# First attention to second layer, taken by halves: the first half of the tokens projected, added and normalised ahead of the second; weight peaks read in eight parts

## The reference

```
h = patches @ W_lin + b, class token, positions                # embedding
z = layernorm(h)
z = z + global_attention(rmsnorm(z, norm1_w))                   # "first attention", 16 heads, latent keys and values, rope
z = z + local_attention(rmsnorm(z, norm2_w))                    # "second layer" of the same block, 4 key heads, rope
h = h + z
n = layernorm(h);  h = h + routed experts(n) (32, best 8) + 2 shared experts(n)
h = h + attention(layernorm(h))                                 # dense, 16 heads
n = layernorm(h);  h = h + quantised MLP(n)
```

## Time and profile before

| what | us |
|---|---|
| median of three runs | 369.97 (368.08 to 370.18) |
| the profiled execution | 369.53 |
| its span, first to last instruction | 367.7 |
| TensorE busy | 348.3 (95%) |
| VectorE busy | 234.3 (64%) |
| ScalarE busy | 192.7 (52%) |
| POOL busy | 135.3 (37%) |

### The profile page before, as it was taken

One profiled execution on the slowest core, in us unless ns is written; L12 is line 12 of the kernel. 1 busy time (PEld: TensorE's weight loads), 2 busy tenths in 40 slices (PEclk: granted clock), 3 DMA queues, 4 the chain that ended last, 5 costly groups with the idle time before them and its releaser, 6 DMA issues.

```text
span 367.7 us, 9982 instructions
## 1 busy us (share of the span) xinstructions
PE 348.3 (95%) x3975; PEld 297.9 (81%) x3975; DVE 234.3 (64%) x507; ACT 192.7 (52%) x384; POOL 135.3 (37%) x144
## 2 busy tenths in 40 slices
PE   8999899998988999999999999999999999889985
PEld 6856666686667999999999999999998688666653
DVE  4546889797769366565556555555555572765787
ACT  5267954686574444445544544445444785232473
POOL 0046752372251356666555544544420012320000
PEclk9999999999999999999999999999999999999999
DMA  8930001000550434353555454544300000000001
GB/s 290 398 139 1 4 4 30 1 4 4 175 173 0 139 112 141 114 151 136 144 150 152 151 141 121 141 142 145 101 0 2 0 2 4 4 6 0 3 0 68
DMA packets 14866, 32.09 MB, mean 87 GB/s; under 512 B 2480, under 2 KB 4464, under 8 KB 14576
## 3 DMA queue, kind: packets, MB, share of 16 engines
q1 hardware_dynamic: 13328, 30.48, 26.0%
q10 hardware_dynamic: 1504, 1.13, 0.9%
HBM read 30.91 MB, written 0.69 MB: 86 GB/s over the span
## 4 chain that ended last, share of the span: by engine, by line
PE 73%; DVE 10%; ACT 8%; issue 5%; DMA 1%; SPq 1%; POOL 1%; POOLq 0%; DVEq 0%; ACTq 0%
PE psum L1172 73%; DMA km<-in_experts 1%; ACT region L797 1%; DVE xn L835 1%; ACT sq L580 1%; ACT region L789 1%; DVE rc L896 1%; SPq L376 1%; DVE nt L830 1%; ACT L567 1%; DVE nt L832 1%; DVE xc L821 1%; ACT region L648 1%; DVE rc L907 1%; ACT ars L583 1%
## 5 line engine op out<-in xcount | busy, mean ns | idle before, releaser
L1172 PE MATMUL psum<-xh,split_all 128*128 128x296 f32 x544 | 122.1, 299 | 0.0
L487 POOL TENSOR_TENSOR split_all<-km,split_all 128x768 fp32r<-128x768 f32 x34 | 62.7, 1848 | 82.0 <-ACT split_all L689 82.0
L1172 PEld LDWEIGHTS psum<-xh,split_all 128*128 128x128 f32 x544 | 91.6, 188 | 0.1
L1172 PE MATMUL psum<-xl,split_all 128*128 128x296 f32 (+1 forms) x288 | 85.1, 300 | 0.6 <-POOL xl L530 0.6
L710 ACT ACTIVATE ah<-rt 128x296 fp32r<-128x296 f32 x64 | 28.9, 452 | 72.9 <-DVE rt L1030 66.2
L1172 PEld LDWEIGHTS psum<-xl,split_all 128*128 128x128 f32 (+1 forms) x288 | 53.1, 187 | 1.6 <-POOL xl L530 1.0
L1172 PE MATMUL psum<-ah,split_all 128*128 128x296 f32 x272 | 48.6, 300 | 1.7 <-ACT ah L710 1.6
L1032 DVE TENSOR_TENSOR al<-rt,ah 128x296 fp32r<-128x296 f32 x60 | 28.7, 478 | 31.1 <-ACT ah L710 31.1
L1027 DVE TENSOR_TENSOR rb<-psum,wb 128x296 f32<-128x296 f32 x60 | 27.9, 466 | 25.1 <-ACT psum L708 24.9
L1172 PEld LDWEIGHTS psum<-ah,split_all 128*128 128x128 f32 x272 | 40.6, 188 | 2.6 <-ACT ah L710 2.0
L1030 DVE TENSOR_TENSOR rt<-rb,psum 128x296 f32<-128x296 f32 x60 | 27.7, 462 | 5.7 <-DVE rb L1027 1.7
(11 more groups left out here) (195 smaller groups left out, 562.8 us busy)
## 6 DMA issues: line engine op xcount, KB each, us to landing
km<-in_experts SPq DMA_DIRECT2D x34, 384.0 KB, 4.0
wb<-weights SPq DMA_DIRECT2D x32, 296.0 KB, 3.7
w_sb<-in_w SPq DMA_DIRECT2D x2, 1024.0 KB, 8.3
region<-in_x SPq DMA_DIRECT2D x6, 296.0 KB, 4.8
region<-in_w_lin ACTq DMA_DIRECT2D x6, 128.0 KB, 5.3
qkv_sb<-in_qkv_w SPq DMA_DIRECT2D x1, 768.0 KB, 4.7
cst<-in_consts SPq DMA_DIRECT2D x1, 502.5 KB, 7.2
out<-x SPq DMA_DIRECT2D x2, 148.0 KB, 1.8
```

The costliest lines, as they stand in the source:

```text
L487: nc.gpsimd.tensor_tensor(wl[i], ring[i], wh[i].bitcast(f32), ALU.subtract)\
L1172: return nc.tensor.matmul(out_, lhsT, rhs, start=start, stop=stop, skip_group_check=True)
```

## The change

The output projection of the first attention is done by halves. The first half's is issued ahead of the value sums of the last pair, into banks 2 and 3; VectorE adds it ahead of the last normalisation. The variance of that half, the projection of the second half (into banks 0 and 1) and eight products for warmth on either side stand in place of `norm(1)`. The second half is squared on ScalarE ahead of `qk_units(1)`; its variance is issued by TensorE after the mean square of unit 0, its root by ScalarE in turn 1 after that turn's copy and square, and its norm is applied by VectorE at the end of turn 1. Each addition is one instruction over both chunks instead of two. The peaks of w1 and w2 are read in eight parts of 512 columns: two after the last normalisation, three after the second half's addition, two and one behind the additions of the second attention, and a small reduction joins them. The core of the diff:

```diff
+PEAK_PARTS = 4
+            def stream_squares(hf):
+                act_e.wait_ge(s_x0, hf + 1)
+                nc.scalar.activation(sq[:, :, half(hf)], x0[:, :, half(hf)], ACT.Square).then_inc(s_sq, 1)
+            def stream_rsqrt(hf):
+                act_e.wait_ge(s_var, 2 + hf + 1)
+                link(nc.scalar.activation(ars[:, half(hf)], ps[2 + hf][:, 0:HALF], ACT.Abs_reciprocal_sqrt,
+                                          bias=eps[:, 2:3]))
+                nc.scalar.activation(nt[:, half(hf)], ars[:, half(hf)], ACT.Square).then_inc(s_ars, 1)
...
+                    if a == 1 and u == 1:
+                        stream_rsqrt(1)
                     if u >= 1:
                         m = n - 1
...
                 if a == 1:
-                    norm(1, mean=False, eps_at=2)
+                    load_table(ACT.Abs_reciprocal_sqrt)
+                    stream_squares(0)
+                    stream_rsqrt(0)
+                    stream_squares(1)
                 qk_units(a)
...
-            def weight_peak(k, w):
-                nc.vector.tensor_reduce(pk[:, k:k + 1], w[:], AX.X, ALU.max, apply_absolute_value=True).then_inc(s_pk, 1)
+            def weight_peak(k, part):
+                n = C * FF // PEAK_PARTS
+                nc.vector.tensor_reduce(pkp[:, k, part:part + 1], (w1_sb, w2_sb)[k][:, part * n:(part + 1) * n], AX.X,
+                                        ALU.max, apply_absolute_value=True).then_inc(s_pkp, 1)
+            def weight_peaks():
+                dve.wait_ge(s_pkp, 2 * PEAK_PARTS)
+                nc.vector.tensor_reduce(pk[:, 0:2], pkp[:], AX.X, ALU.max).then_inc(s_pk, 2)
...
                         ins.then_inc(s_kmv, 1)
+                    if a == 1 and u == 1:
+                        norm_apply(1, 4, 2, (1,))
...
+            def stream_added(hf):
+                dve.wait_ge(s_wo, hf + 1)
+                dve.wait_ge(s_x0s, hf + 1)
+                nc.vector.tensor_tensor(x0[:, :, half(hf)], x0[:, :, half(hf)],
+                                        psum[:, 2 - 2 * hf:4 - 2 * hf, 0:HALF], ALU.add).then_inc(s_x0, 1)
...
-                if a == 1:
-                    norm_apply(1, 4, 2)
                 qk_units(a)
+                if a == 0:
+                    for p in range(PAIRS - 1):
+                        normalise_grouped(0, p)
+                    stream_added(0)
+                    normalise_grouped(0, PAIRS - 1)
+                    dve.wait_ge(s_ffw, 32)
+                    weight_peak(0, 0)
+                    weight_peak(0, 1)
+                    norm_apply(1, 4, 2, (0,))
+                    stream_added(1)
+                    weight_peak(0, 2)
+                    weight_peak(0, 3)
+                    weight_peak(1, 0)
+                    continue
...
-                    ins.then_inc((s_x0, s_h)[a], 1)
-                if a == 0:
-                    weight_peak(1, w2_sb)
+                    ins.then_inc(s_h, 1)
+                    if hf == 0:
+                        weight_peak(1, 1)
+                        weight_peak(1, 2)
+                    else:
+                        weight_peak(1, 3)
+                        weight_peaks()
...
                     exchange(a, u)
+                    if a == 1 and u == 0:
+                        pe.wait_ge(s_x0, 2)
                     head_mean_squares(a, u)
+                    if a == 1 and u == 0:
+                        stream_variance(1)
...
-            def project_grouped(a):
-                for hf in range(2):
-                    pe.wait_ge(s_on, a * PAIRS + PAIRS // 2 * (hf + 1))
+            def project_grouped(a, hf):
+                pe.wait_ge(s_wo_w, 16 * (a + 1))
+                pe.wait_ge(s_on, a * PAIRS + PAIRS // 2 * (hf + 1))
...
+            def stream_variance(hf):
+                pe.wait_ge(s_sq, 2 + hf + 1)
+                for c in range(C):
+                    ins = mm(ps[2 + hf][:, 0:HALF], const("mean"), sq[:, c, half(hf)], c == 0, c == C - 1)
+                ins.then_inc(s_var, 1)
...
+                        if p == PAIRS and a == 0:
+                            project_grouped(0, 0)
                         grouped_values(a, p - 1)
...
                 if a == 1:
-                    norm(1, mean=False)
+                    keep_busy(7, 8)
+                    stream_variance(0)
+                    project_grouped(0, 1)
+                    keep_busy(7, 8)
                     pe.wait_ge(s_attn_w[1], 48)
                 qk_units(a)
```

More of the change, by code:

```diff
@@ L204, in program @@
         pk1 = sb("pk1", [P, 4])
+        pkp = sb("pkp", [P, 2, PEAK_PARTS])
         scale = sb("scale", [P, 4])
@@ L314, in program @@
         s_pk = sem("peaks_ready")
+        s_pkp = sem("peak_of_a_part_of_the_weights_read")
         s_pkb = sem("peaks_on_all_partitions")
@@ L823, in centre, with norm_apply @@
                         .then_inc(s_cent, 1)
-            def norm_apply(n, count, eps_at=0):
-                for hf in range(2):
+            def norm_apply(n, count, eps_at=0, halves=range(2)):
+                for hf in halves:
                     dve.wait_ge(s_ars, count + hf + 1)
@@ L940, in _ @@
             for a in range(2):
-                if a == 1:
-                    norm_apply(1, 4, 2)
                 qk_units(a)
+                if a == 0:
[12 more added lines that the diff above has]
+                    continue
                 for p in range(PAIRS):
-                    normalise_grouped(a, p)
-                if a == 0:
-                    dve.wait_ge(s_ffw, 32)
-                    weight_peak(0, w1_sb)
+                    normalise_grouped(1, p)
                 for hf in range(2):
[L950 to L954, removed]
+                    dve.wait_ge(s_wo, 2 + hf + 1)
+                    dve.wait_ge(s_hx, hf + 1)
                     for m in range(C):
-                        y = (x0, h)[a][:, m, half(hf)]
+                        y = h[:, m, half(hf)]
                         ins = nc.vector.tensor_tensor(y, y, ps[4 + 2 * m + hf][:, 0:HALF], ALU.add)
-                    ins.then_inc((s_x0, s_h)[a], 1)
-                if a == 0:
-                    weight_peak(1, w2_sb)
+                    ins.then_inc(s_h, 1)
[5 more added lines that the diff above has]
+                        weight_peaks()
             centre(2)
@@ L1352, in weighted_values @@
                 ins.then_inc(s_o, 1)
-            def project_grouped(a):
-                for hf in range(2):
-                    pe.wait_ge(s_on, a * PAIRS + PAIRS // 2 * (hf + 1))
[L1358 to L1362, removed]
+            def project_grouped(a, hf):
+                pe.wait_ge(s_wo_w, 16 * (a + 1))
+                pe.wait_ge(s_on, a * PAIRS + PAIRS // 2 * (hf + 1))
+                for m in range(C):
+                    bank = 2 - 2 * hf + m if a == 0 else 4 + 2 * m + hf
+                    for c in range(C):
+                        ins = mm(ps[bank][:, 0:HALF], wo_sb[:, c, m * P:(m + 1) * P],
+                                 ot4[:, c, half(hf)], c == 0, c == C - 1)
+                ins.then_inc(s_wo, 1)
+            def stream_variance(hf):
+                pe.wait_ge(s_sq, 2 + hf + 1)
+                for c in range(C):
+                    ins = mm(ps[2 + hf][:, 0:HALF], const("mean"), sq[:, c, half(hf)], c == 0, c == C - 1)
+                ins.then_inc(s_var, 1)
             def project_out():
@@ L1495, in _ @@
                 attention(a)
-                pe.wait_ge(s_wo_w, 16 * (a + 1))
-                project_grouped(a)
+                if a == 1:
+                    for hf in range(2):
+                        project_grouped(1, hf)
             norm(2)
```

## The result

The changed kernel takes 372.91 us (median of 20 executions, 369.80 to 374.39) against 369.72 for the kernel before beside it (20 executions). The ratio is 1.0077, with a 95% interval of 1.0060 to 1.0095: slower by 2.2 to 3.5 us. The forecast was 371.2 in a range of 368.9 to 373.5, no change by the bound of 1% its likeliest class. The time lies in the range and the class came as forecast; but a rival that had been given 1 in 10 is part of the result. The traced execution, at 374.39, is the slowest of the 20, so its trace may show more than the median does.

What follows compares the result with a forecast made beforehand. Bound: a chain hopping between engines at the attention layers' join, then TensorE's unbroken 14.43 us. First half gains 2.8, but the second half's stall nets +1.6; with +0.1 for peaks, 369.53 becomes 371.2 us, range 368.9 to 373.5.

Steps and rivals of the forecast that it cites:

- a rival that had been given 1 in 10: TensorE's clock falls to 1.2 GHz in the pause before the second half's projection: two units +4.0, 375.2 us; chance 0.10.
- First half: Join of the attention layers: early output projection and addition start the second layer's first projection at 62.7 against 65.52, gain 2.8.
- Second half: Its first projection waits for VectorE's normalisation behind unit 1's steps: 72.2 against 70.58, +1.6, and all later units follow.
- the stall: Main case: TensorE waits over 3 us for the normalised second half, costing +1.6; 371.2 us in all; chance 0.82.
- The sum: Whole kernel: +1.6 at the join and +0.1 behind the second attention, +1.7 on 369.53, giving 371.2 us.
- The +0.1 behind the second attention: Last peak part and combining step delay VectorE's centring by 0.1 to 0.3, mostly covered by ScalarE's expert weights; +0.1 taken.

Runs made afterwards that it cites:

- the second profile of the change: The changed kernel, unaltered, run again in a later set beside the kernel before: 372.45 us, ratio 1.0094.
- 12 products: The changed kernel with 12 more products for warmth at the head of TensorE's pause before the second half's first projection: 369.81 us, ratio 1.0028.
- the parts alone: The kernel before with only the weight peaks in eight parts, the halves of the output projection kept together: 368.91 us, ratio 0.9962.
- the variance first and POOL held: Change with second half's norm before unit 1, its variance before unit 0's exchange, POOL's unit 0 sum held until that norm: 365.81 us, again 368.46.

## Why the prediction was right in its class, and where it was off

**First half: right.** 62.7 was forecast; it is 62.99 from a start 0.5 later, and 62.50 in the second profile of the change. VectorE's addition fell at 57.13 (56.8 forecast) and the peaks stood hidden under the waits, 0.6 to 0.7 each as taken.

**Second half: right in place, order and size.** Unit 1's first step at 68.75 (68.5), the projection at 72.56 and 72.07 (72.2), TensorE waiting 3.35 for line 855. One term was short: the step of line 852 took 0.70, not the 0.47 inside the 1.98 taken from the earlier trace rows, because in the trace of before POOL did nothing beside it and here its product for unit 1 ran. (Unit 1's four steps were added up as 1.7 where the rows give 1.8; they took 1.69, 68.75 to 70.44.)

**The clock: the step that failed.** It stood as a rival to the stall, with 0.10 and "against it: the stretch ahead of the pause is dense, and eight products for warmth stand twice just before". What the runs show is not a rival but the stall's companion: the fall came in spite of the dense stretch, and the products for warmth do not stand just before: the later eight end near 63.0, 6 us ahead of the pause. Of the 20 executions three kept a mean clock of 1.000, at 369.80 to 369.85; the one at 0.998 took 371.32, all others 372.0 or more. That most executions had this fall is read from those times, not from the mean clock: of the 86 executions of the kernel before in the later sets 73 lie below 1.000 as well, and the 28 below 0.995 have a median of 370.1 against 369.5 for the 31 at 0.998 or more. Its price was taken as 4.0, two units at twice their length; it is 2.7 to 2.8 in the trace, since the clock came back near 78.1, after 5.6 us of work at half the pace. In the time it is 2.6 in the one set that has both the change and a kernel that kept the clock in its trace (372.45 against 369.81 with 12 products). The Trainium skill, "TensorE: Matmul & The Clock Gate", section "Why this matters for your kernels", warned of such a pause, and the trace agrees: 3.35 us of it, and a clock of 0.50.

**The sum.** +1.7 was forecast and +2.8 measured by the ratio, +3.5 in the second set. Stall and clock together are 4.3 in both profiles of the change once the later start is taken off (81.46 - 76.66 - 0.5; the value sums at 80.95 in the second). The stall alone, with the clock kept by products in the pause, is 1.6 in both traces (78.75 - 76.66 - 0.5; 78.13 - 76.66 + 0.1), which is the term that was forecast. So that the time lies in the range is luck in part: the sum left the clock out, 2.7 in the trace, and the executions that gave the result show 1.5 less than the trace does (0.8 less in the second set). Why they show less was not tried. Two things in the rows may bear on it. Not every execution need have all of the stall and of the clock. And the base is one execution: its first attention ended 0.4 to 0.7 earlier than in eight of the twelve later traces. TensorE's wait for no cause that the profile shows, ahead of the last but one scores, was 0.38 in it (51.64), and 0.64 to 0.93 in eight of the others; on the other hand its expert loop took 146.48, where five later profiles show 145.5. So a walk along one trace, good to 0.3 us at the join, was worth some 1 us in the time.

**The peaks.** The +0.1 behind the second attention was 0.3 on TensorE (from the mean's product to the variance 3.05, 104.99 to 108.04, against 2.75, 100.50 to 103.25), and the parts alone do not make it. Their own gain, 1.4 by the ratio (0.9962 of 370), had no term of its own in the sum. Had the sum been split, it would have shown that the parts gain without the halves; the halves without the parts were not run.

**A second fall of the clock** stands in the trace of the change at 115.6 to 119, at a clock of 0.50:

```profile
116.00:119.00 3.00, 3.00 (x12) 2.84 (x12) 2.79 (x28) 1.68 (x3) 0.00 (x0) 0.50 0.00 0
```

Four of the other traces have one near there, that of the parts alone among them. It costs nothing: from the first product of the experts to their loop it is 22.04 here (115.36 to 137.40), and 22.02 to 22.06 in all thirteen traces, with such a fall or without. In the trace of before TensorE waits 1.16 for ScalarE a little later (ahead of 116.23); here the slow products fill that wait. No pause like the first stands ahead of this fall: TensorE's last waits were 0.90 (ahead of 108.04) and 0.43 (ahead of 114.00). Its cause is open.

## What to carry to other kernels

Splitting a join by halves moves its wait to where the second half is first needed; look for the engine whose queue the second half stands in, and issue its steps as soon as their input is ready, even ahead of the first half's next steps; here that took the wait from 3.35 to 1.57 and, with the variance first and POOL held, to 0.19. A wait of TensorE costs its length, and the slow clock behind it where the clock falls: here it held through 1.8 us, fell in 3.35 and cost 2.7 more in the trace, and a dozen idle products in the pause took that away. Cut long reductions into pieces that fit the waits before moving anything else: that alone gained 0.7 to 2.1 us here, and no order of the halves was shown to be faster than that.

## What was not expected of the hardware

VectorE's steps with two inputs in SBUF are stretched when POOL runs: lines 852 and 855 took 0.77 and 1.27 beside POOL's two products, 0.47 and 0.78 without them, while line 850, one of whose inputs is in PSUM, took 0.52 both times. The stretched steps end (69.07 and 70.37) 0.32 and 0.64 after POOL's products do (68.75 and 69.73), as if each had begun only 0.14 to 0.15 ahead of that. The Trainium skill, "SBUF — State Buffer", section "Who interferes with whom", says that a VectorE instruction with two SBUF inputs contends with a GpSimd instruction that reads SBUF, that the ports the two engines share are an exclusive lock, and that the order of issue decides who waits; the trace agrees.
